# Cross-attention with 16 heads of 8: row maxima from stacks of 48 rows, two heads at a time in the halves of TensorE's array

## The reference, cut to what matters

```python
q = q.reshape(B, SQ, 16, 8).transpose(0, 2, 1, 3) * SCALE
k = k.reshape(B, SKV, 16, 8).transpose(0, 2, 1, 3)
v = v.reshape(B, SKV, 16, 8).transpose(0, 2, 1, 3)
scores = jnp.einsum('bhqd,bhkd->bhqk', q, k)
attn = jax.nn.softmax(scores, axis=-1)
ctx = jnp.einsum('bhqk,bhkd->bhqd', attn, v)
return ctx.transpose(0, 2, 1, 3).reshape(B, SQ, HIDDEN) @ Wo.T + bo
```

## Time and profile before

| what | value |
|---|---|
| median of 3 runs | 2919.11 us (2916.24 to 2924.52) |
| the profiled execution | 2919.91 us, its span 2918.1 us |
| mean granted clock of TensorE in it | 0.87 |
| PE, PEld, DVE, ACT, POOL busy | 80%, 53%, 54%, 45%, 26% of the span |
| L0x, L1x, L3x stand at | 152 to 475, 995 to 1326, 2463 to 2816 us |

### The profile page before, as it was taken

One profiled execution on the slowest core, in us unless ns is written; L12 is line 12 of the kernel. 1 busy time (PEld: TensorE's weight loads), 2 busy tenths in 40 slices (PEclk: granted clock), 3 DMA queues, 4 the chain that ended last, 5 costly groups with the idle time before them and its releaser, 6 DMA issues. The chain is left out here.

```text
span 2918.1 us, 49184 instructions
## 1 busy us (share of the span) xinstructions
PE 2344.6 (80%) x16209; PEld 1534.3 (53%) x16238; DVE 1589.7 (54%) x4946; ACT 1306.9 (45%) x3187; POOL 751.3 (26%) x1054
## 2 busy tenths in 40 slices
PE   6969895667887389883478999876969997899989
PEld 4624443644554234442366777555847775455553
DVE  4757773145556587762215555363447775777730
ACT  4715553124455135553424666532326654255442
POOL 0122211533232422200373333114621112222100
PEclk9969996858888578896688999997989998699989
DMA  2022225220000032213160000125420000322200
GB/s 74 2 75 85 81 66 153 51 72 15 30 30 15 27 87 78 78 38 101 50 124 12 2 1 2 44 68 141 146 86 1 2 2 21 92 73 75 63 17 15
DMA packets 131357, 160.30 MB, mean 55 GB/s; under 512 B 23171, under 2 KB 93452, under 8 KB 129957
## 3 DMA queue, kind: packets, MB, share of 16 engines
q1 hardware_dynamic: 115528, 132.84, 15.7%
q0 software_dynamic: 12976, 23.22, 3.0%
q10 hardware_dynamic: 2624, 1.32, 0.3%
HBM read 120.82 MB, written 37.79 MB: 54 GB/s over the span
## 5 line engine op out<-in xcount | busy, mean ns | idle before, releaser
L725 DVE CUSTOM_DVE_ANT_0 L3x_ps_ring<-L3x_ps_ring,L3x_mask_q 128x512 f32<-128x512 f32 x256 | 174.0, 709 | 68.0 <-PE L3x_ps_ring L960 53.5
L728 DVE TENSOR_REDUCE L0x_mx<-L0x_ps_ring 128x1 f32<-128x512 f32 x256 | 166.8, 686 | 70.7 <-PE L0x_ps_ring L960 69.9
L728 DVE TENSOR_REDUCE L1x_mx<-L1x_ps_ring 128x1 f32<-128x512 f32 x256 | 166.1, 686 | 61.9 <-PE L1x_ps_ring L960 61.0
L856 ACT ACTIVATE L3x_p_ring<-L3x_ps_t 128x1024 f32<-128x1024 f32 x128 | 131.1, 1025 | 146.0 <-PE L3x_ps_t L999 145.8
L856 ACT ACTIVATE L1x_p_ring<-L1x_ps_t 128x1024 f32<-128x1024 f32 x128 | 130.4, 1025 | 121.4 <-PE L1x_ps_t L992 120.7
L856 ACT ACTIVATE L0x_p_ring<-L0x_ps_t 128x1024 f32<-128x1024 f32 x128 | 130.4, 1025 | 105.6 <-PE L0x_ps_t L992 105.1
L1368 ACT ACTIVATE L2a_probs<-L2a_ps_s,L2a_top 128x256 f32<-128x256 f32 x256 | 118.0, 473 | 93.2 <-DVE L2a_top L1318 92.3
L992 PE MATMUL L3x_ps_t<-L3x_q_stack,L3x_k_stack 75*128 75x256 bf16 x512 | 124.6, 279 | 5.5 <-ACT L3x_p_ring L856 5.4
L960 PE MATMUL L1x_ps_ring<-L1x_k_stack,L1x_q_stack 72*128 72x512 bf16 x256 | 103.8, 430 | 30.3 <-DVE L1x_mx L728 16.4
L960 PE MATMUL L0x_ps_ring<-L0x_k_stack,L0x_q_stack 72*128 72x512 bf16 x256 | 103.1, 428 | 29.2 <-DVE L0x_mx L728 15.6
L999 PE MATMUL L3x_ps_t<-L3x_mask_k,const_ident_bf 128*128 128x256 bf16 x512 | 124.3, 279 | 0.0
(11 more groups left out here) (687 smaller groups left out, 6134.7 us busy)
## 6 DMA issues: line engine op xcount, KB each, us to landing
L0x_k_stack<-L0x_k_dram SPq DMA_DIRECT2D x96, 96.0 KB
L1x_k_stack<-L1x_k_dram SPq DMA_DIRECT2D x96, 96.0 KB
L3x_k_stack<-L3x_k_dram SPq DMA_DIRECT2D x96, 96.0 KB
L0f_w<-L0f_in_w SPq DMA_DIRECT2D x32, 256.0 KB, 7.9
L1a_rk_wide<-L1a_rk_dram SPq DMA_DIRECT2D x8, 1024.0 KB, 4.6
L1f_w<-L1f_in_w SPq DMA_DIRECT2D x32, 256.0 KB, 3.2
kept_x<-ctxT SPq DMA_DIRECT2D x24, 256.0 KB, 3.2
L0x_q_stack<-L0x_q_dram SPq DMA_DIRECT2D x96, 48.0 KB
```

Source lines behind the costliest of these rows:

```text
L725: dve.tensor_tensor_reduce(bank, bank, mask_q[:, qt, :], 1.0, 2 * MASKED, ALU.add, ALU.max, accum_out=mx[:, qt, h:h + 1]).then_inc(took_se ...
L728: dve.tensor_reduce(mx[:, qt, h:h + 1], bank, AX, ALU.max).then_inc(took_sem(n), 1)
L856: act.activation(pr, pt, ACT.Exp, scale=scale).then_inc(exp_done.sem, 1)
```

## The change

Maxima are taken from stacks of their own, `q_top` and `k_top`, with 48 rows for a head: six products of parts instead of nine, large with large, middle and small, middle with large and middle, small with large. A pair of heads stands in one column block of the tile, the even head in rows 0 to 47, the odd head in rows 64 to 111. For that, the parts are stored in another arrangement (`q_dram` and `k_dram` have six places and two copies by batch parity; three stores each for q and k instead of two and one).

A slot now holds the maxima matmuls of two heads for one tile of queries, one right after the other: slots 2i and 2i + 1 make heads 2i and 2i + 1 for tiles 0 and 1. What stood between the two matmuls of a slot comes after both. Before the first of a pair, PE waits for the banks of both. Loads of the tops (`tops`, four DMAs a quarter) take the places of the loads of the full stacks; those are issued in slots 2, 4, 6 and 9 for the next batch. The full scores wait for them in each fourth slot; POOL's split waits for the stores and no longer for the stacks' loads.

```diff
+TOP_ROWS = 48
...
+            q_top = sb("q_top", [P, H // 2, S], BF16)
+            k_top = sb("k_top", [P, H // 2, nkeys], BF16)
...
+            elif small:
+                items += [("s", (h // 2 * 2, h % 2), "dve"), ("s", (h // 2 * 2 + 1, h % 2), "dve")]
...
-            after_scores = {0: [("negate", 1, 0)], 1: [("ln", 0, 2)], 3: [("outputs", 3, -1)], 7: [("outputs", 0, 0)],
+            after_scores = {0: [("negate", 1, 0)], 1: [("ln", 0, 2)], 2: [("stack", 0, 1)], 4: [("stack", 1, 1)],
+                            6: [("stack", 2, 1)], 9: [("stack", 3, 1)], 3: [("outputs", 3, -1)], 7: [("outputs", 0, 0)],
                             8: [("negate", 0, 1)], 12: [("outputs", 1, 0)], 15: [("outputs", 2, 0)]}
...
-            at_end = {1: [("ln_rest", 0, 2), ("stack", 3, 1), ("values_first", 3, -1)], 2: [("item", item("x"), 2)],
+            at_end = {1: [("ln_rest", 0, 2), ("tops", 3, 1), ("values_first", 3, -1)], 2: [("item", item("x"), 2)],
                       3: [("item", item("v"), 1)], 5: [("split", 0, 2), ("values_first", 0, 0)], 9: [("add", 0, -1)],
-                      10: [("item", item("m", 0), 1)], 11: [("stack", 0, 2)], 12: [("stack", 1, 2)], 13: [("stack", 2, 2), ("values_first", 2, 0)]}
+                      10: [("item", item("m", 0), 1)], 11: [("tops", 0, 2)], 12: [("tops", 1, 2)], 13: [("tops", 2, 2), ("values_first", 2, 0)]}
...
-                slots.append(("item", first[u, 0], 1))
+                slots += [("item", first[u // 2 * 2 + j, u % 2], 1) for j in range(2)]
                 slots += between.get(u, [])
-                slots.append(("item", first[u, 1], 1))
                 slots += at_end.get(u, [])
...
                         wait_step(sp, q_split, b, 4)
-                        sp.dma_start(q_dram[0:3].rearrange("i p k -> p i k"), parts["q"][:]).then_inc(q_stored.sem, 16)
-                        sp.dma_start(q_dram[3:5].rearrange("i p k -> p i k"), parts["q"][:, 0:2, :]).then_inc(
-                            q_stored.sem, 16)
+                        for first, last, taken_from in ((0, 3, 0), (3, 5, 0), (5, 6, 0)):
+                            sp.dma_start(q_dram[par, first:last].rearrange("i p k -> p i k"),
+                                         parts["q"][:, taken_from:taken_from + last - first, :]).then_inc(q_stored.sem, 16)
                         wait_step(sp, k_split, b, 4)
-                        sp.dma_start(k_dram[:].rearrange("i p k -> p i k"), parts["k"][:]).then_inc(k_stored.sem, 16)
+                        for first, last, taken_from in ((0, 3, 0), (3, 5, 1), (5, 6, 2)):
+                            sp.dma_start(k_dram[par, first:last].rearrange("i p k -> p i k"),
+                                         parts["k"][:, taken_from:taken_from + last - first, :]).then_inc(k_stored.sem, 16)
...
+                    if kind == "tops":
+
+                        if not (isinstance(b, int) and b < 1):
+                            made(sp, b - 1, last_top(k))
+                            wait_step(sp, tops_in[k], b, 0)
+                        pairs = slice(QUARTER // 2 * k, QUARTER // 2 * (k + 1))
+                        wait_step(sp, q_stored, b, 48)
+                        for j in range(2):
+                            sp.dma_start(q_top[64 * j:64 * j + TOP_ROWS, pairs],
+                                         q_dram[par].rearrange("i (d n j) k -> j (i d) n k", n=H // 2, j=2)[j][:, pairs]
+                                         ).then_inc(tops_in[k].sem, 16)
...
-                        for quarter in stacked:
-                            wait_step(pool, quarter, b, 0)
+                        wait_step(pool, q_stored, b, 0)
+                        wait_step(pool, k_stored, b, 0)
...
+                            if small and h % 2 == 0:
+
+                                other, other_back = previous(n + 1, b)
+                                if other is not None:
+                                    taken(pe, b - other_back, other)
...
-                                wait_step(pe, stacked[h // QUARTER], b, 6 * 16)
-                            queries = q_stack[0:MAX_ROW, par, h, :] if small else qm[:, par, h, :]
-                            keys = k_stack[0:MAX_ROW, par, h, :] if small else kT[:, par, cfg["kchunk"](h), :]
+                                wait_step(pe, tops_in[h // QUARTER], b, 4 * 16)
+                            half_rows = slice(64 * (h % 2), 64 * (h % 2) + TOP_ROWS)
+                            queries = q_top[half_rows, h // 2, :] if small else qm[:, par, h, :]
+                            keys = k_top[half_rows, h // 2, :] if small else kT[:, par, cfg["kchunk"](h), :]
...
+                        if small and u % QUARTER == 0:
+                            wait_step(pe, stacked[u // QUARTER], b, 6 * 16)
```

34 lines of the change are left out of this document (23 added, 11 removed).

## The result

| what | before | after |
|---|---|---|
| median, us | 2917.68 (2912.14 to 2924.52, 4 runs) | 2966.28 (2964.83 to 2967.2, 4 runs) |
| profiled execution: span, clock | 2918.1, 0.87 | 2963.7, 0.858 |

The kernel after takes 1.0165 of the time of before, 95% interval 1.0142 to 1.0188: 48.6 us slower. The forecast was 2932 with a range up to 2957. The sign was right; the time is 34 us above the forecast and 9 above the range. All ratios are of fast executions alone: two slow ones are left out, 3622.86 us of the order with the wait and 3009.24 us of 64 rows with short maxima.

A forecast was written before the change was run, and what follows sets the result against it. PE's in-order instruction stream was taken to set these layers, DVE not far behind. -26 + 22 + 10 + 2 + 5 = +13 us on 2919.9 gave 2933, median 0.8 lower: 2932 us, range 2901 to 2957.

The forecast's parts named there:

- The pairs and switches: PE's stream, 21 passes: 3.4 us a pass saved by paired matmuls, 2.3 paid for 25 more switches; -26 us.
- The clock: Passes of L0x and L1x: 0.3 more stretches a pass at the lower clock from more short waits; +5 us.
- signs that the prediction set for being wrong: L3x stays at 37.5, batches of L0x fall under 31.5 us, or clock and batch time move together.
- The rival that the clock decides: One 3.4 us stretch more at the lower clock in each of 21 passes, 25 instead of 5; 2955, chance 0.10.
- The two-bank wait: PE waits for both banks before a pair: +1.35 us a pass in L0x and L1x, +0.4 in L3x; +22 us.
- The pass ahead and the DMAs: Maxima-only pass of each layer, DVE-bound, loses 3.3 us: +10 us; first maximum 0.7 later a layer: +2 us.
- the walk: Step through slots with traced durations; pair cycle without an item in the pass ahead 1.42 us against 1.22 of DVE work.
- the store of the maxima behind the stacks: On SP, behind twelve stack-load issues: 0, covered by the longer pass ahead; 1 to 2 us a layer if not longer.
- 1.0 of waits before that go: Slots 2 to 10 of a pass: 1.0 us of old waits disappears, set against 2.35 of new waits.

The follow-up runs named there:

- the order with the wait: Kernel before with the new item order and the wait for both banks ahead of each pair, on 72 rows and the full array; 1.0172 of before.
- 64 rows with short maxima: Kernel before with the new item order, maxima matmuls on 64 of 72 rows in series, DVE maxima over every second column; 1.0007 of before.
- the transfers: Kernel before with the new item order and all stores and loads of the change, the tops unread, maxima still from 72 rows; 0.9978 of before.
- own waits: Kernel after without the two-bank wait, each matmul waiting for its own bank only; 1.0072 of before.
- the second run of own waits: Kernel after without the two-bank wait, run again; 1.0124 of before.
- runs with short maxima: DVE maxima over every second column, in four kernels: new order alone 0.9771, that with 64 rows in series 1.0007, after without two-bank wait 0.991, after 0.993.
- the runs in series: Kernel before with the new item order, maxima matmuls on 64 or 48 of 72 rows, one after the other in one half; 1.0307 and 1.0381 of before.
- the order: Kernel before with the new item order alone, 72-row stacks and own-bank waits kept; 0.9943 of before.
- the second run: Kernel before with the new item order alone, run again; 0.9993 of before.

## Why the prediction was wrong, point by point

**The pairs and switches: the step that failed, by size.** -26 us was forecast, as 3.4 saved less 2.3 paid a pass. Each local price held: 0.09 to 0.10 a switch, two matmuls in one's time, and the traces have the 25 more changes of shape that were counted (16 and 41 in a pass). What failed is the step from the saved matmul time to the time of the pass. The prediction itself had read how little room DVE leaves, used it for the new wait, and then counted every 0.215 of the pairs as time won. At full clock pairs and switches together make -0.07 us a pass in L3x, and +0.3 in L0x (32.09 against 31.79) and L1x (32.95 against 32.70). Over 21 passes that is about +3 instead of -26. By the layers' table the step from the transfers to own waits is even 15 us slower, and 34 with the second run of own waits, but that has the moved stacks and the clock in it. The runs with short maxima show that DVE's time is half of the reason in L3x; in L0x most of the reason is open.

**The clock: right sign, far too small.** +5 was forecast for all of it. After has 340 us at 1.2 GHz in the three layers, before 257. Leaving out what stands ahead of the first scores, it is 186 against 129. At the estimated 0.41 us each these 57 us cost 23 (21 to 30). Two of the signs that the prediction set for being wrong came true: L3x does not fall below 37.5, and clock and batch time move together. The rival that the clock decides (2955) is the nearest of all. The prediction expected more time at 1.2 GHz from more short waits of PE; the runs in series show that the shape of the matmuls does it without new waits. Whether that is also what lowers the clock of after, where the pairs run at once, is likely but not separated: L1x's five passes had 14 us at 1.2 GHz with the transfers and 34 with the pairs, and are 8.5 us longer for it.

**The two-bank wait: cause right, size in the passes too large.** 22 us were forecast for the passes, 10 for the passes ahead. L3x pays 0.86 a pass for 0.4, and it vanishes when DVE is faster, as its cause demands. In L0x and L1x, compared at the same clock, a pass pays some 0.2 for 1.35: L0x at 0.86 has 36.27, 36.17, 36.36 and 36.21 with own waits and 36.35 and 36.54 in after; L1x at 0.90 has 35.67 and 35.59 against 35.89 and 35.70. Together that is about 9 us (an estimate) instead of 22. From the first run of own waits to after the layers' table has 33.0, almost the 32 that were forecast, but this is luck: after is 46 us longer at 1.2 GHz. From the second run, with the same time at 1.2 GHz, it has 13.7.

**The pass ahead and the DMAs: right.** For the passes ahead 10 us were forecast; they grew by 13.4, of which 2.5 come with the order, which had no price. Pair to pair takes 1.46 us there in after (203.06 to 204.51), against 1.42 in the walk. The first maximum of a layer waits 12.08, 12.13 and 12.13 us instead of 11.83, 11.73 and 12.03: 0.8 in the three layers together for 2. For the store of the maxima behind the stacks the prediction took 0, as the longer pass ahead covers it, and 1 to 2 a layer if it does not. Both came true: after has no wait for it at its first scores, and own waits lose 1.9 us a layer.

**The order: not priced.** The three layers are 14 us shorter with it (13 in the second run), the whole kernel 0.1 to 0.6%, and 10 to 12 of the 14 can be the clock. The prediction counted "1.0 of waits before that go" only as a discount on the new wait.

Added up by place, after against before: 13 us in the passes ahead, some 6 in the 21 passes at the same clock (0.45 in L3x, some 0.2 in the others), some 23 by the clock, 42 in all. The forecast by the same places: 12, -4 (-26 + 22) and 5. So of the 29 us that are missing in the layers, the clock makes 18 and the passes 10. In the passes larger errors stand against each other: 29 us too much gained by the pairs, 13 us too much paid for the wait, and the order, which had no term. That they show so little in the sum is luck, and so, in part, is the right sign. By part, the pairs' term is the largest error.

## What to carry to other kernels

Time saved on an engine counts only where that engine is late; if another stands close behind it, price the saving and the new wait by the same walk, not one by its sum and the other by its place. A smaller matmul is not a cheaper one: here a shape that uses half of the array paid for two changes of shape at 0.10 us each and, in two layers of three, for a lower clock. For a layer's start, follow both chains that let the first result go, the maxima on DVE and their round trip: only the one that ends last costs, and taking a wait out of one uncovers the other. And before two sums are compared, compare the clock in them: here the same kernel differed by 19 us between two chips.

## What the hardware showed unexpectedly

- The shape of one group of matmuls moves TensorE's clock. 64 of 72 rows, nothing else changed, took L0x and L1x from passes of 32 to 36 us to passes of 33 and of 46 to 50, with 44.3 us of PE's records in one of 45.8. So here the lower clock was granted to a PE that waits for almost nothing; less work in each matmul gave a longer kernel by 3 to 4%.
- L3x, with the same shapes and PE busy for 37.8 us of a pass of 39.2, stays at 2.4 GHz in its five passes between output projections, in every one of these kernels. What tells it from L0x (128-row mask matmuls between the scores, as one difference) was not tried.
- A single store issued behind twelve loads landed 1.0 us later than without them (2.47 against 1.43 until the load that waits for it is issued), which shows only where someone waits for it: 2.20 us at L0x's first scores with own waits, nothing in after.
